# Causal attention: the mask products of the row maxima are 128 columns wide instead of 128 to 512

## What is computed

```python
def _L0_xattn_ref(query, key_value, Wq, bq, Wk, bk, Wv, bv, Wo, bo):
    ...
    scores = jnp.einsum('bhqd,bhkd->bhqk', Q, K) / np.sqrt(HEAD_DIM)
    causal = jnp.tril(jnp.ones((SQ, SKV), bool))
    scores = jnp.where(causal[None, None], scores, -jnp.inf)
    attn = jax.nn.softmax(scores, axis=-1)
    out = jnp.einsum('bhqk,bhkd->bhqd', attn, V)
    out = out.transpose(0, 2, 1, 3).reshape(B, SQ, D_MODEL)
    return out @ Wo.T + bo
```

## Time and profile before

| | us |
|---|---|
| median of 3 runs | 3201.78 |
| lowest and highest run | 3201.13, 3211.98 |
| the profiled execution | 3196.11 |
| its span, first to last instruction | 3194.4 |
| the causal attention's maxima and scores, within the span | about 492 to 956 |

### The profile page before, as it was taken

One profiled execution on the slowest core, in us unless ns is written; L12 is line 12 of the kernel. 1 busy time (PEld: TensorE's weight loads), 2 busy tenths in 40 slices (PEclk: granted clock), 3 DMA queues, 4 the chain that ended last, 5 costly groups with the idle time before them and its releaser, 6 DMA issues. The chain is left out here.

```text
span 3194.4 us, 83729 instructions
## 1 busy us (share of the span) xinstructions
PE 2806.6 (88%) x34974; PEld 1416.8 (44%) x34975; DVE 2064.1 (65%) x4240; ACT 1568.5 (49%) x2122; POOL 224.4 (7%) x295
## 2 busy tenths in 40 slices
PE   6677987999996997799999999999999999369993
PEld 3465552444534564134434343443433333246662
DVE  4335136888855235688999898988998995312224
ACT  2223222666672322266767776776666768123331
POOL 2001201000001002300000000000000000210003
PEclk9888997999997999699999999999999999589997
DMA  5322023011001003312112112111111110611102
GB/s 155 102 60 67 27 72 100 13 39 39 3 2 37 1 0 109 99 42 67 34 53 51 53 36 60 44 44 51 42 49 44 44 44 2 249 49 33 33 31 89
DMA packets 112871, 173.46 MB, mean 54 GB/s; under 512 B 17882, under 2 KB 88427, under 8 KB 112147
## 3 DMA queue, kind: packets, MB, share of 16 engines
q1 hardware_dynamic: 109460, 160.11, 17.5%
q0 software_dynamic: 3072, 8.39, 0.8%
HBM read 127.63 MB, written 40.51 MB: 53 GB/s over the span
## 5 line engine op out<-in xcount | busy, mean ns | idle before, releaser
L1304 DVE TENSOR_REDUCE d_part_max<-d_ps_m 128x1 f32<-128x512 f32 (+1 forms) x1964 | 1128.1, 631 | 89.0 <-PE d_ps_m L1291 52.7
L1612 ACT ACTIVATE d_prob<-d_ps_s 128x1024 f32<-128x1024 f32 x928 | 898.7, 1022 | 345.7 <-PE d_ps_s L1481 338.9
L1291 PE MATMUL d_ps_m<-k_st,q_st 97*32 97x512 bf16 (+1 forms) x5296 | 479.2, 361 | 20.5 <-DVE d_part_max L1304 16.9
L1481 PE MATMUL d_ps_s<-q_st,k_st 98*32 98x512 bf16 x5104 | 439.5, 382 | 9.7 <-ACT d_prob L1612 8.4
L690 DVE TENSOR_REDUCE x_part_max<-x_att_ps_m 128x1 f32<-128x512 f32 (+2 forms) x578 | 309.6, 587 | 50.2 <-PE x_att_ps_m L675 22.7
L936 ACT ACTIVATE x_att_prob<-x_att_ps_s 128x1024 f32<-128x1024 f32 (+3 forms) x296 | 258.8, 920 | 138.8 <-PE x_att_ps_s L817 82.8
L1499 PE MATMUL d_ps_o<-d_prob,a_values 128*32 128x512 f32 x2048 | 265.0, 592 | 0.0
L1291 PEld LDWEIGHTS d_ps_m<-k_st,q_st 97*32 97x32 bf16 x5296 | 141.5, 95 | 274.2 <-DVE d_part_max L1304 127.8
L1291 PE MATMUL d_ps_m<-q_st 97*32 97x512 bf16 (+1 forms) x2560 | 230.9, 361 | 2.2 <-DVE d_part_max L1304 0.4
L1481 PEld LDWEIGHTS d_ps_s<-q_st,k_st 98*32 98x32 bf16 x5104 | 136.6, 97 | 196.0 <-issue 82.4
L1499 PE MATMUL d_ps_o<-d_prob,x_values 128*32 128x512 f32 x1664 | 215.5, 593 | 0.4 <-ACT d_prob L1612 0.4
(11 more groups left out here) (326 smaller groups left out, 3344.8 us busy)
## 6 DMA issues: line engine op xcount, KB each, us to landing
k_st<-parts_k SPq DMA_DIRECT2D x90, 256.0 KB, 5.5
k_st<-parts_k SPq DMA_DIRECT2D x90, 208.0 KB, 4.4
l_w<-in_l_w SPq DMA_DIRECT2D x16, 1024.0 KB, 14.1
q_st<-parts_q SPq DMA_DIRECT2D x48, 256.0 KB, 4.7
q_st<-parts_q SPq DMA_DIRECT2D x192, 64.0 KB
q_st<-parts_k SPq DMA_DIRECT2D x30, 256.0 KB
q_st<-parts_k SPq DMA_DIRECT2D x30, 208.0 KB
parts_q<-a_proj_parts SPq DMA_DIRECT2D x16, 384.0 KB, 2.5
```

What stands on the lines that cost most here:

```text
L1291: mm = pe.matmul(bank[q:q + COLUMNS, 0:w], self.query(s, h, ROW_MASK + 1, a * P + q, COLUMNS), self.key(s, h, ROW_MASK + 1, k, w), start=T ...
L1304: dve.tensor_reduce(self.part[:, h * QT + a, i:i + 1], bank[:, 0:w], AX.X, ALU.max).then_inc(s_read, 1)
L1481: mm = pe.matmul(ps_s[u][k:k + COLUMNS, hh, :], maxima.key(s, h, ROW_MAX + 1, kt * P + k, COLUMNS), maxima.query(s, h, ROW_MAX + 1, 0, QC) ...
L1612: act.activation(prob[:, p % 2, 2 * u:2 * u + 2, :], ps_s[u][:, :, :], ACT.Exp, scale=scale).then_inc(s_prob, 1)
```

## The change

The constant `causal_q` becomes 128 columns wide and holds the diagonal square alone. The mask quad of the causal kind uses all of it and writes the last 128 columns of the chunk (`bank[:, w - P:w]`). The band kind's mask is as before. The number and the order of instructions on every engine are the same; only widths differ. One source line less stands in `prepare`, so that a line of the kernel after has a number that is smaller by one.

```diff
-    c["causal_q"] = sb("causal_q", [P, QC], BF16)
+    c["causal_q"] = sb("causal_q", [P, P], BF16)
...
-            off = QC - P
             fill(c["causal_k"][:, :], 0.0)
             select(c["causal_k"][:, :], ALU.is_ge, NEG, 0, [[1, P]], -1)
             fill(c["causal_q"][:, :], 0.0)
-            select(c["causal_q"][:, :], ALU.is_ge, NEG, off, [[-1, QC]], 1)
+            select(c["causal_q"][:, :], ALU.is_ge, NEG, 0, [[-1, P]], 1)
...
         if masked:
             if at.kind == "band":
-                m = cst["band_q"][:, k - t * P + BAND:k - t * P + BAND + w]
+                m, edge = cst["band_q"][:, k - t * P + BAND:k - t * P + BAND + w], out
             else:
-                m = cst["causal_q"][:, QC - w:QC]
+                m, edge = cst["causal_q"][:, :], bank[:, w - P:w]
             for q in range(0, P, COLUMNS):
-                mm = pe.matmul(out[q:q + COLUMNS, :], cst["ident_bf"][:, q:q + COLUMNS], m, start=False, stop=True,
+                mm = pe.matmul(edge[q:q + COLUMNS, :], cst["ident_bf"][:, q:q + COLUMNS], m, start=False, stop=True,
                                skip_group_check=True)
```

## The result

| | before | after |
|---|---|---|
| median of 20 runs each, us | 3202.12 | 3196.39 |
| lowest and highest run | 3198.76, 3211.98 | 3190.92, 3201.13 |
| the profiled execution | 3196.11 | 3200.2 |
| maxima entries under the projections, in the trace | 54.3 | 52.4 |
| causal attention, first score product to the output product | 409.6 | 404.4 |

The ratio of the times is 0.9976, with a 95% interval of 0.9968 to 0.9983: 7.7 us less (5.4 to 10.2). It is real and smaller than 0.5%.

What follows compares the result with a forecast made beforehand. The prediction took PE to set the pace in the attention stage's long stretch. It summed 10.0 us there and 2.5 us in the projection to 12.5 us off the median 3201.8, giving 3189.3 us, range 3179 to 3203.

Steps and rivals of the forecast that it cites:

- The price of a narrow quad: On PE, a 128-column mask quad costs its columns, 0.05 us to the next start; its four weight loads overlap the quad before.
- Rival 2: A narrow quad costs more than its columns: a set of mask quads saves 0.16 us, half the forecast; 3195.5 us; chance 0.08.
- Before the turn, 0.32 in full: Attention, 605 to 608.7 us: one set of mask quads saves 0.32 us, kept in full in three periods.
- Between turn and wait, 0.37 lost: Attention, 608.7 to 613.5 us: the 0.37 us saved only lengthens PE's DMA wait from 1.45 to 1.82, three times.
- The long stretch "kept in full": Attention, 613.5 to 650 us: nearly 7 sets save 2.19 us, kept in full three times, 6.6 us.
- The stretch after it, "two thirds": Attention, 650 to 675 us and its like: 0.96 us in four places, 3.8 us, of which two thirds, 2.5, count.
- The attention stage, 10.0: Causal attention: of 12.5 us removed from PE, 10.0 us are kept and 2.4 lost.
- The projection stage, 2.5: Maxima entries in the projection stage: 2.5 us less, between 0 and 4.4, partly from shorter DVE waits for mask quads.
- Constants, nothing: Constants: POOL fills 128 instead of 512 columns and saves some tenths of a us, which cost and gain nothing.
- Rival 1: DVE's hand-over decides: only its waits for mask quads count, 5.2 us in attention and 1.3 in projection; 3195.3 us; chance 0.16.
- Rival 4: Slower: more PE idling in projection and the three DMA waits makes the clock fall earlier or more often; 3211 us; chance 0.04.
- Rivals 3 and 5: Rival 3: every column counts, 17 us off, 3184.8 us, chance 0.10; rival 5: the edit does nothing, 3201.8 us, 0.02.

Runs made afterwards that it cites:

- attend_only: The kernel before with the narrow mask product in the attention stage alone; ratio 0.9979 to before, attention stage 402.2 us.
- turn2: The kernel after with each causal turn two entries after the last maximum instead of four; ratio 0.9956 to before, attention stage 398.4 us.
- turn2_wide: The kernel before with each causal turn two entries after the last maximum instead of four; ratio 0.9988 to before, attention stage 405.8 us.
- no_mask: The kernel after without the causal mask quads of the maxima products; ratio 0.9966 to before, attention stage 399.9 us.
- even_load_wide: The kernel before with causal entries placed by DVE's estimated load against PE's estimated time, not by count; ratio 1.0025 to before, attention stage 418.7 us.
- double_wide: The kernel before with every causal mask quad of the maxima issued twice at full width; ratio 1.0070 to before, attention stage 427.5 us.
- project_only: The kernel before with the narrow mask product in the projection stage alone; ratio 0.9998 to before, projection stage 52.2 us.
- turn1: The kernel after with each causal turn one entry after the last maximum instead of four; ratio 0.9982 to before, attention stage 403.1 us.
- half_reduce_wide: The kernel before with DVE reducing half of each causal maxima chunk and the scale at 1/64, for times alone; ratio 0.9948, attention stage 399.3 us.
- half_reduce: The kernel after with DVE reducing half of each causal maxima chunk and the scale at 1/64, for times alone; ratio 0.9913, attention stage 390.8 us.
- even_turn2: The kernel after with causal turns two entries after the last maximum and entries placed by estimated load; ratio 0.9991 to before, attention stage 410.9 us.
- even_load: The kernel after with causal entries placed by DVE's estimated load against PE's estimated time, not by count; ratio 0.9981 to before, attention stage 410.7 us.

## Why the prediction was right and wrong

The time, 3196.39, lies in the range, and the difference is under 0.5%, as the likeliest case said. That was not hard to meet: the range of 3179 to 3203 also holds the time of no change, 3202.12. The forecast's size, 12.5 us, is outside the interval of 5.4 to 10.2, and the term that was sized wrong is the attention stage's, 10.0 for a measured 7.4. Step by step:

- **What bounds the stage**: right. The period shrank with DVE's busy time unchanged, and added columns cost 74% of their time in the three periods.
- **The price of a narrow quad**: right. It is 0.06 us from start to start behind four weight loads. Rival 2 falls. Its rule of 25 ns is that of the Trainium skill, "TensorE: Matmul & The Clock Gate", section "Wait — 56ns, not 53.3ns?": by it four matmuls would take 0.10 us, and the trace does not agree. My 13 ns are a mean, not a spacing: the four matmuls of a mask quad start within 11 ns in the median, before and after, and the next quad starts 0.06 us behind the first of them.
- **Before the turn, 0.32 in full**: right in two periods out of three (0.22 in the first, 0.33, 0.32).
- **Between turn and wait, 0.37 lost**: right. The wait went from 1.45 to 1.84, and the stretch kept its length.
- **The long stretch "kept in full"**: wrong in size. Up to 642.4 (and its like) 1.87 us were on offer per period and 1.55, 1.55 and 1.45 came in attend_only, 1.1 us less in all. I read a PE without a gap as a PE on which everything counts. What takes the 0.3 to 0.4 us is open; it is not DVE's load, as with half of that 1.58 came.
- **The stretch after it, "two thirds"**: too high as well. From 642.4 to the fourth turn I had 0.32 + 0.64 = 0.96 of 1.28 us, and 0.59, 0.57 and 0.91 came: 0.8 us less in all. Here the reason was the one I named, PE held by the banks: with the half-loaded DVE 1.00 came.
- **The attention stage, 10.0**: measured 7.4 where no fall of the clock stands behind the three waits (attend_only, and the pair turn2 and turn2_wide). Beside the two steps above, 0.5 us went behind the fourth wait, where the mask plays no part, and 0.3 in small pieces.
- **The projection stage, 2.5**: measured 1.9 to 2.1. DVE waits less often for mask quads, as predicted; that this alone makes the 2 us was not shown.
- **Constants, nothing**: nothing in the traces contradicts it; it wasn't tried by itself.
- **Rival 1, DVE's hand-over**: 6.5 us is nearer to the ratio's 7.7 than my number, but for another reason. It put the gain into DVE's waits for mask quads, 22.7 us in 49 waits. They shrank to 18.4 us in 35 in attend_only: 4.3 us, while the stage shrank by 7.4. What is true of it is that DVE takes its part where the banks run out, between the third and the fourth turn.
- **Rival 4, the clock**: rejected as a whole, present on a small scale. In the projection stage of after the clock did not fall earlier. But a fall came behind one of the three longer waits, at 1.2 us, where I had estimated 2. Together with the later return at the stage's start (0.75) it took 2.0 us of the 7.4 in the trace of after. And a fall was there all along: the fourth wait, 2.19 us, has one behind it in before too, while I had argued from the stretch with the first wait alone.
- **Rivals 3 and 5**: neither. Nothing near 17 us came, and more than nothing did.

So the sum is 7.4 + 2.1 = 9.5 us in traces without a fall behind the three waits, and 7.7 by the runs, whose interval holds both. The clock's 2.0 us in after's own trace would explain the difference; how often the clock falls in other executions can't be read from one trace each.

## What to carry to other kernels

A gap-free engine gives back less than it is relieved of (60% in the three periods of no_mask), and costs more of what is added (74%): don't take a saving as kept because the engine has no gap (here 59% of the narrow product's columns came back in the stage where I had summed 80%), and read where its neighbour is nearly full apart from where it is not. A saving ahead of a fixed DMA latency only lengthens the wait for it, so look at what starts that DMA: moving the turn two entries earlier was worth 3.8 us, half as much as the change itself, and one entry more lost 4.7. And compare stages, and medians of many runs, where one profiled execution may be 6 us off its own median. Within a stage, set aside the stretches where the clock's return or a fall differs: here they moved single results by 1 to 6 us.

## What was unexpected of the hardware

- Idle spells of TensorE as short as 1.76 us (the third wait of even_load_wide) were followed by a fall of the granted clock to half (1.2 GHz) for a part of the next 6 to 7 us, in some cases and not in others:

| the wait, us | kernels | clock below 1.00 in the 7 us behind it |
|---|---|---|
| 0.69 to 0.79 | double_wide, turn2_wide | 0 of 6 |
| 1.21 to 1.45 | before, project_only, turn2, turn1, half_reduce_wide | 0 of 15 |
| 1.60 to 1.70 | half_reduce | 0 of 3 |
| 1.75 to 1.85 | after, attend_only, even_load_wide | 2 of 9 |
| 2.01 to 2.02 | even_turn2 | 1 of 3 |
| 2.12 to 2.13 | even_load | 3 of 3 |
| 2.23 to 2.24 | no_mask | 2 of 3 |
| 2.19 to 2.22 | the fourth wait, all 14 kernels | 14 of 14 |

The mean clock of those 7 us was 0.76 behind the first three waits each time, and 0.57 to 0.76 behind the fourth. A fall cost 0.9 to 1.2 us where the same work stood beside it at full clock. Waits of one length end both ways, so the length alone does not decide, and no row here tells what else does.
- Four matmuls of 128 columns in different 32-column strips took 0.06 us from the start of one quad to the start of the next, with four weight loads in between: some 14 ns for each matmul. The weight loads, 0.11 us in flight, added nothing to it.
- DVE stood still for 2.35 to 2.64 us at one place of the second group in all 14 kernels, with nothing in the profile that it waited for. In three of them the clock fell behind it, and the stretch took 4.8 to 6.4 us more than its like.
- Executions of one kernel differ by 10 us (3190.92 to 3201.13 in 20 runs of after). In the two traces that were compared, stages that the change doesn't touch took more time where their mean granted clock was lower.
